# Two layers of attention and routed experts on one core: the sums between the layers move to GpSimd, and the gating work of layer 1 is spread over four units of its attention

## What is computed

```python
x = L0_attn_hidden_states                      # 4 x 512 x 256
xn = layernorm(x)
x = x + L0_attn(xn) + L0_ffn(xn)               # 16 experts, best 4 of each token, and a shared one
xn = layernorm(x)
x = x + L1_attn(xn) + L1_ffn(xn)               # 32 heads in 8 groups; 7 experts, best 3, and a shared one

# L1_attn, for each batch and each of 8 groups g with 4 heads of size 8
sim = q[g, r] @ k[g].T / sqrt(8)
out[g, r] = softmax(sim) @ v[g]
# L1_ffn: gating
probas = softmax(x @ gate_w + gate_b); take the best 3 of (probas + biases)
```

## Time and profile before

| | us |
|---|---|
| median of 3 runs | 1141.22 |
| the 3 runs | 1140.10, 1141.22, 1143.67 |
| span of the profiled execution, first to last instruction | 1136.1 |
| TensorE busy in it | 1018.1 (90%) |
| VectorE busy | 762.7 (67%) |
| ScalarE busy | 604.8 (53%) |
| GpSimd busy | 317.4 (28%) |

### The profile page before, as it was taken

One profiled execution on the slowest core, in us unless ns is written; L12 is line 12 of the kernel. 1 busy time (PEld: TensorE's weight loads), 2 busy tenths in 40 slices (PEclk: granted clock), 3 DMA queues, 4 the chain that ended last, 5 costly groups with the idle time before them and its releaser, 6 DMA issues.

```text
span 1136.1 us, 17535 instructions
## 1 busy us (share of the span) xinstructions
PE 1018.1 (90%) x5780; PEld 743.6 (65%) x5780; DVE 762.7 (67%) x1591; ACT 604.8 (53%) x911; POOL 317.4 (28%) x331
## 2 busy tenths in 40 slices
PE   4998898779999846799999999999999997999995
PEld 3877776669999724555555555555555565888884
DVE  6576454556655346798899888888888846444437
ACT  6325445355565543466665666666666665444431
POOL 2005777066655500000000122222221000455441
PEclk9999999989999967899999999999999998999999
DMA  6863333354444272011111222222222124333253
GB/s 231 315 263 126 124 110 120 113 195 150 136 124 135 89 305 35 14 28 29 29 29 29 43 55 57 56 56 57 56 56 43 63 73 155 108 108 101 92 196 137
DMA packets 49140, 120.49 MB, mean 106 GB/s; under 512 B 7752, under 2 KB 24904, under 8 KB 48520
## 3 DMA queue, kind: packets, MB, share of 16 engines
q1 hardware_dynamic: 36096, 82.80, 25.5%
q0 software_dynamic: 11808, 32.37, 7.5%
q10 hardware_dynamic: 1152, 4.19, 0.9%
HBM read 72.30 MB, written 52.42 MB: 110 GB/s over the span
## 4 chain that ended last, share of the span: by engine, by line
PE 65%; DVE 16%; POOL 7%; issue 4%; ACT 3%; DMA 3%; SPq 0%; ACTq 0%; DVEq 0%; POOLq 0%
PE psum L817 11%; PE psum L838 9%; PE psum L826 7%; DVE work_f L1699 6%; POOL xg L466 5%; PE psum L633 5%; PE psum L634 4%; PE psum L635 4%; PE psum L547 3%; PE psum L548 3%; PE psum L549 3%; PE psum L619 3%; PE psum L644 2%; DVE x L1310 1%; PE psum L665 1%
## 5 line engine op out<-in xcount | busy, mean ns | idle before, releaser
L1699 DVE TENSOR_REDUCE work_f<-psum 128x1 f32<-128x512 f32 x512 | 337.3, 685 | 49.1 <-PE psum L817 46.7
L1203 ACT ACTIVATE work_f<-psum 128x1024 f32<-128x1024 f32 x172 | 169.5, 1023 | 104.9 <-PE psum L826 100.5
L817 PE MATMUL psum<-work_r 128*128 128x512 f32 x512 | 207.8, 445 | 18.9 <-DVE work_f L1699 7.0
L473 POOL DMA_INDIRECT yk<-yb,dest x134 | 131.3, 980 | 240.1 <-ACT yb L1057 206.7
L817 PEld LDWEIGHTS psum<-work_r 128*128 128x128 f32 x512 | 93.4, 190 | 133.8 <-DVE work_f L1699 71.2
L826 PE MATMUL psum<-qm,work_r 128*128 128x512 f32 x512 | 160.8, 396 | 0.9 <-ACT work_f L1203 0.8
L466 POOL DMA_INDIRECT xg<-xn,slot x112 | 108.2, 966 | 180.9 <-PE psum L853 143.5
L826 PEld LDWEIGHTS psum<-qm,work_r 128*128 128x128 f32 x512 | 93.8, 188 | 24.1 <-ACT work_f L1203 6.2
L633 PE MATMUL psum<-wexp,xbh 128*128 x268 | 102.1, 381 | 7.4 <-issue 7.2
L1203 ACT ACTIVATE pt<-psum 128x1024 f32<-128x1024 f32 x84 | 82.8, 1022 | 45.9 <-PE psum L826 42.7
L634 PE MATMUL psum<-wexp,xbh 128*128 x268 | 96.4, 360 | 0.0
(11 more groups left out here) (218 smaller groups left out, 2065.2 us busy)
## 6 DMA issues: line engine op xcount, KB each, us to landing
xb<-xg SPq DMA_DIRECT2D x67, 258.0 KB
xg<-in_pad SPq DMA_DIRECT2D x1, 10320.0 KB
yg<-yk SPq DMA_DIRECT2D x20, 512.0 KB, 9.0
stage<-in_moe SPq DMA_DIRECT2D x16, 608.0 KB
xg<-in_pad SPq DMA_DIRECT2D x1, 7224.0 KB
work_r<-work_r SPq DMA_DIRECT2D x128, 48.0 KB
work_r<-work_r SPq DMA_DIRECT2D x32, 192.0 KB
stage<-in_moe SPq DMA_DIRECT2D x16, 384.0 KB, 3.7
```

The lines of the kernel that those rows point to most:

```text
L473: nc.gpsimd.indirect_dma_start(yk[l], bass.IndirectOffsetOnAxis(ap=dest[:, j % 8, i:i + 1], axis=0), yb[l][:, j % 2, i, :], None).then_inc ...
L817: nc.tensor.matmul(next_bank(pe, ("scores", n), b_mx, n + 1), qs[g % 2][:, t * P:(t + 1) * P], km[g % 4][:, r, :], start=True, stop=True). ...
L1203: nc.scalar.activation(pt[((b * NG + g) * QT + t) % 3][:, 2 * h:2 * h + 2, :], psum[:, 3 + 2 * h:5 + 2 * h, :], ACT.Exp, scale=float(HD) * ...
L1699: v.reduce_max(mx[:, s % 2, i:i + 1], ring["scores", n], AX.X).then_inc(b_mx, 1)
```

## The change

1. Batch 0: GpSimd adds choice 3 to choice 2; VectorE adds choices 0, 1 and then that sum to `x`.
2. Batch 1: as before, but TensorE's sum is made in two halves with `tokens_t(1, 0)` between them.
3. Batches 2 and 3: GpSimd makes four additions of 128 x 1024 each (`sum_choices`), the last onto `x`. TensorE's sums of these batches are gone.
4. All three projections of batch 0 stand one after the other ahead of stage (0, 0); ScalarE splits the first two before it normalises batch 1. VectorE's `root(1, 1)` stands behind its `clear()`.
5. The tokens' transposes of batches 2 and 3 are in the ring, one bank at a time, in stages (0, 1) and (0, 2); the logits of batches 0 to 3 and their transposes stand one batch at a time in stages (0, 0) to (0, 3). No stage waits for all of them. `lt[1]` holds two batches in place of four. The routing steps begin in stage (0, 4) and not in (0, 3).

```diff
+            def sum_choices(b):
+                y = yg[0][b]
+                pool.wait_ge(m_yg[b], 16 * TOP0)
+                nc.gpsimd.tensor_tensor(y[:, 1], y[:, 1], y[:, 2], ALU.add).then_inc(q_sum, 1)
+                nc.gpsimd.tensor_tensor(y[:, 3], y[:, 3], y[:, 0], ALU.add).then_inc(q_sum, 1)
+                pool.wait_ge(q_sum, choice_sums(b) - 1)
+                nc.gpsimd.tensor_tensor(y[:, 1], y[:, 1], y[:, 3], ALU.add).then_inc(q_sum, 1)
+                pool.wait_ge(q_sum, choice_sums(b))
+                tiles = slice(b * QT, (b + 1) * QT)
+                nc.gpsimd.tensor_tensor(x[:, tiles, :], x[:, tiles, :], y[:, 1], ALU.add).then_inc(q_x, 1)
-            for b in range(B):
-                root(1, b)
+            pool.wait_ge(m_yg[0], 16 * TOP0)
+            nc.gpsimd.tensor_tensor(yg[0][0][:, 2], yg[0][0][:, 2], yg[0][0][:, 3], ALU.add).then_inc(q_sum, 1)
+            root(1, 0)
+            pool.wait_ge(s_xb, TT)
+            pool.wait_ge(f_y, batches(0, B))
+            sum_choices(2)
+            root(1, 1)
+            sum_choices(3)
+            root(1, 2)
+            root(1, 3)
...
             # TensorE
-            sum_results(1, 4)
+            sum_results(0)
             tokens_t(1, 0)
-            sum_results(2, 6)
+            sum_results(1).then_inc(m_ps, 1)
             pe.wait_ge(s_split, SPLIT_A1)
             pe.wait_ge(s_xl, 2 * B + 2)
             project(2, 0, psum[:, 0, :])
             project(0, 0, psum[:, 2, :])
-            pe.wait_ge(s_ve, B + 2)
-            sum_results(3, 4)
-            pe.wait_ge(b_hi, 1)
-            tokens_t(1, 1)
+            project(1, 0, psum[:, 6, :])
+            pe.wait_ge(b_lo, 2)
...
-            stage(0, 0, False, {1: lambda: pe.wait_ge(s_xl, 2 * B + 4), 3: last_projection, 7: lambda: tokens_t(1, 2),
-                                11: lambda: tokens_t(1, 3), 12: first_values})
-            pe.wait_ge(s_xl, 2 * B + 8)
-            for b in range(B):
-                logits(1, b, psum[:, 4 + b, :])
-            logits_by_token(1)
-            pe.wait_ge(s_lc, 2)
-            stage(0, 1, False)
-            sequence(0, False)
+            stage(0, 0, False, {3: lambda: tokens_t(1, 1), 6: lambda: first_logits(0), 9: first_values,
+                                10: lambda: logits_by_token1(0), 13: lambda: first_logits(1)})
+            pe.wait_ge(s_xl, 2 * B + 4)
+            stage(0, 1, False, {1: lambda: logits_by_token1(1), 3: lambda: tokens_t1(2, 0), 6: lambda: tokens_t1(2, 1),
+                                14: lambda: first_logits(2)})
+            stage(0, 2, False, {3: lambda: tokens_t1(3, 0), 5: lambda: logits_by_token1(2), 6: lambda: tokens_t1(3, 1),
+                                14: lambda: first_logits(3)})
+            stage(0, 3, False, {5: lambda: logits_by_token1(3)})
...
             # ScalarE
             normalised(1, 0)
             high_parts(1, 0)
-            normalised(1, 1)
             compact(2, 0, psum[:, 0, :], 0)
             compact(0, 0, psum[:, 2, :], 1)
+            normalised(1, 1)
+            compact(1, 0, psum[:, 6, :], 2)
             high_parts(1, 1)
+            logits(1, 0, ring["logits", 0])
             normalised(1, 2)
+            logits(1, 1, ring["logits", 1])
+            act.wait_ge(q_sum, choice_sums(3))
+            stage(0, 1, False, {(0, 1): lambda: high_parts1(2, 0), (1, 0): lambda: high_parts1(2, 1),
+                                (3, 0): lambda: normalised(1, 3), (3, 1): lambda: logits(1, 2, ring["logits", 2])})
+            stage(0, 2, False, {(0, 1): lambda: high_parts1(3, 0), (1, 0): lambda: high_parts1(3, 1),
+                                (3, 1): lambda: logits(1, 3, ring["logits", 3])})
...
             # VectorE
-            combine0(0, 0)
+            dve.wait_ge(m_yg[0], 16 * TOP0)
+            add_choice(0, 0)
+            add_choice(0, 1)
+            dve.wait_ge(q_sum, 1)
+            add_choice(0, 2)
+            noted()
             moments(1, 0)
             root(1, 0)
-            combine0(1, 4)
+            dve.wait_ge(m_yg[1], 16 * TOP0)
+            add_choice(1, 0)
             low_parts(1, 0)
-            moments(1, 1)
-            root(1, 1)
+            dve.wait_ge(m_ps, sums(0, 1))
+            noted()
+            note(add_to_tokens(slice(QT, 2 * QT), 4))
...
             compact(2, 0, psum[:, 0, :], 0)
+            moments(1, 1)
             compact(0, 0, psum[:, 2, :], 1)
             clear()
             v.memset(rec[:], 0.0).then_inc(b_on, 1)
+            root(1, 1)
...
+            stage(0, 0, False, {4: lambda: compact(1, 0, psum[:, 6, :], 2), 6: lambda: low_parts(1, 1),
+                                8: lambda: moments_of(2), 11: lambda: root(1, 2),
+                                12: lambda: take_logits1(0), 14: lambda: values_by_key(0, psum[:, 7, :])})
+            stage(0, 1, False, {3: lambda: take_logits1(1), 5: lambda: low_parts1(2, 0), 8: lambda: low_parts1(2, 1),
+                                9: lambda: moments_of(3), 12: lambda: root(1, 3)})
+            stage(0, 2, False, {5: lambda: low_parts1(3, 0), 7: lambda: take_logits1(2), 8: lambda: low_parts1(3, 1)})
+            stage(0, 3, False, {7: gate})
```

More of the change, by code:

```diff
@@ L558, in tokens_t, with tokens_t1, logits_by_token1 @@
                     ins.then_inc(s_xnT, 1)
+            def tokens_t1(b, k):
+                pe.wait_ge(s_xn, TT + (b + 1) * QT)
+                o = next_bank(pe, ("tokens", b, k), s_xl, 2 * B + KH * b + k + 1)
+                for t in range(QT):
+                    ins = nc.tensor.transpose(o[:, t * P:(t + 1) * P], xn[1][:, b * QT + t, k * P:(k + 1) * P], ident)
+                ins.then_inc(s_xnT, 1)
+            def logits_by_token1(b):
+                pe.wait_ge(s_lt, B + b + 1)
+                o = next_bank(pe, ("logits by token", b), s_lc, 2 + b)
+                for t in range(QT):
+                    ins = nc.tensor.transpose(o[:, t * P:(t + 1) * P], lt[1][:, b % 2, t * P:(t + 1) * P], ident)
+                ins.then_inc(s_lx, 1)
             def logits(layer, b, o):
@@ L1008, in normalised, with high_parts1 @@
                                          bias=rs[:, 7, t:t + 1]).then_inc(s_xn, 1)
+            def high_parts1(b, k):
+                act.wait_ge(s_xnT, 2 * B + b * KH + k + 1)
+                copy(xt_hi[1][:, k, b * S:(b + 1) * S], ring["tokens", b, k]).then_inc(s_xh, 1)
             def logits(layer, b, o):
                 act.wait_ge(s_lg, layer * B + b + 1)
-                copy(lt[layer][:, b, :], o).then_inc(s_lt, 1)
+                if layer and b < 2:
+                    act.wait_ge(q_x, 1)
+                if layer and b >= 2:
+                    act.wait_ge(s_lx, b)
+                copy(lt[layer][:, b % 2 if layer else b, :], o).then_inc(s_lt, 1)
             def gating_exp(ne, count, n):
@@ L1188, in outputs, with stage @@
                 copy(ot[:], psum[:, 7, :]).then_inc(b_ot, 1)
-            def stage(b, s, last):
+            def stage(b, s, last, early={}):
                 back, following = s >= 1, not last and s >= 1
                 for t in range(QT):
-                    if isinstance(b, int) and (b, s, t) == (0, 2, 1):
-                        gating_exp(E1, 2, TT)
                     if back:
@@ L1208, in stage, with both @@
                     outputs(b, s - 1)
+            def both(*steps):
+                return lambda: [step() for step in steps]
             normalised(1, 0)
             high_parts(1, 0)
-            normalised(1, 1)
             compact(2, 0, psum[:, 0, :], 0)
             compact(0, 0, psum[:, 2, :], 1)
+            normalised(1, 1)
+            compact(1, 0, psum[:, 6, :], 2)
             high_parts(1, 1)
+            logits(1, 0, ring["logits", 0])
             normalised(1, 2)
-            compact(1, 0, psum[:, 3, :], 2)
-            high_parts(1, 2)
-            normalised(1, 3)
-            high_parts(1, 3)
-            for b in range(B):
-                logits(1, b, psum[:, 4 + b, :])
-            stage(0, 1, False)
-            for s in range(2, NG + 2):
+            logits(1, 1, ring["logits", 1])
[4 more added lines that the diff above has]
+                                (3, 1): lambda: logits(1, 3, ring["logits", 3])})
+            stage(0, 3, False, {(3, 0): lambda: gating_exp(E1, 2, TT)})
+            for s in range(4, NG + 2):
                 stage(0, s, False)
@@ L1507, in routed, with add_choice @@
                     weights(j)
-            def combine0(b, bank):
-                dve.wait_ge(f_y, batches(0, b + 1))
-                dve.wait_ge(s_xb, TT)
-                dve.wait_ge(m_yg[b], 16 * TOP0)
+            def add_choice(b, k):
                 tiles = slice(b * QT, (b + 1) * QT)
-                for k in range(1 if b else TOP0):
-                    noted()
-                    note(v.tensor_tensor(x[:, tiles, :], x[:, tiles, :], yg[0][b][:, k], ALU.add))
-                if b:
-                    dve.wait_ge(m_ps, sums(0, b))
-                    noted()
```

(15 more changed lines are left out.)

80 lines of the change are left out of this document (44 added, 36 removed).

## The result

The changed kernel takes 1146.6 us in the median of 5 runs (1145.55 to 1148.22) against 1140.1 of the kernel before (5 runs, 1138.75 to 1143.67). The ratio is 1.0057, with a 95% interval of 1.0043 to 1.007: slower, and above the range of 1131 to 1145. The span of the profiled execution went from 1136.1 to 1143.7 us. What lies around the instructions is 1.8 us (1145.55 for the execution with the span of 1143.7), not the 5.1 given ahead of the prediction, so the profiled execution of before took an estimated 1137.9 and was a quick one: the 7.6 us between the spans are more than the 6.5 between the medians.

What follows compares the result with a forecast made beforehand. VectorE's sums, statistics and low parts were taken to set the first stage, then a wait for TensorE's gating block. Head +1.6, stage (0, 0) -7.7, block and later stages summed to -3.3 us: 1137.9 from 1141.2, range 1131 to 1145.

Steps and rivals of the forecast that it cites:

- Step 1: Batch 0's additions: three on VectorE and one on GpSimd, one after the other, take 6.1 us; costs 1.1.
- Step 2: Batch 0's statistics and roots up to the projections: TensorE projects at 425.7, before 426.1.
- the toss: Whether batch 0's last root instruction, due at 418.4, passes GpSimd's additions from 418.3; if caught, 2.2 to 4.5 us later.
- Step 3: Head, projections: the key split no longer stands behind 2.08 us of ScalarE; first score at 437.0, before 438.6.
- Step 4: End of head: VectorE's root of batch 1 waits on GpSimd's additions, 6.5 us; first maximum at 441, before 439.4.
- Step 5: Stage (0, 0): takes 19 us, its last maximum at 460, before 466.1.
- case D: Rival: nine places in the three-bank ring cost 2.0 us each; stages (0, 1) to (0, 3) over 52, total 1146; chance 0.15.
- Step 7: Stage (0, 2): added tokens and logits cost 3.0 us, bounds 1.4 and 5.4; ends at 493.3, before 497.7.
- step 8: Stage (0, 3): 14.4 us, ending at 507.6, before 511.4; routing steps paid one stage later, 0.5.
- Step 6: Stage (0, 1): 17.0 us, 1.0 of it waiting for ScalarE's copy; ends at 477.0, before 484.4.
- B: Rival: VectorE is let in beside GpSimd's additions, so the first maximum comes 4.5 us sooner; 1133.5; chance 0.23.
- C: Rival: batch 0's root is caught at 418.4 and held to 423.2, +3.5 us; 1141.5, no change seen; chance 0.18.

Runs made afterwards that it cites:

- e1_hold: The changed kernel, but GpSimd waits for VectorE's roots of batches 0 and 1 before its next sums; 1.0013 of the kernel before.
- e7_logits: The changed kernel with only the logits' copies of batches 2 and 3 moved ahead of ScalarE's exponential (3, 0); 1.0032 of the kernel before.
- e6_tokens: The changed kernel with only the first token copy of batches 2 and 3 moved ahead of ScalarE's exponential (0, 0); 1.003 of the kernel before.
- e5_three: The changed kernel with GpSimd waiting for VectorE's roots, the exponential table loaded early, and token and logits copies ahead of the exponentials; 0.9933 of the kernel before.
- e11_no_logits: e5_three without the logits of batches 2 and 3, their turned form, copies and additions; 0.9911 of the kernel before.

## Why the prediction was wrong, step by step

**Step 1, right.** Batch 0's additions ended 5.87 us after the landing (6.1 predicted). The timeline of after, head:

```profile
408.08 2.34 POOL L542 TENSOR_TENSOR yg<-yg 128x1024 f32<-128x1024 f32 x1 [9.63 <-DMA yg<-yk]
408.22 5.87 DVE L1572 TENSOR_TENSOR x<-x,yg 128x1024 f32<-128x1024 f32 x3 [16.61 <-DMA yg<-yk]
...
418.25 3.36 POOL L533 TENSOR_TENSOR yg<-yg 128x1024 f32<-128x1024 f32 x1 [0.98 <-DMA yg<-yk]
...
432.43 2.34 POOL L533 TENSOR_TENSOR yg<-yg 128x1024 f32<-128x1024 f32 x1
433.84 0.95 DVE L1337 TENSOR_TENSOR rs<-rs 128x4 f32<-128x4 f32 x1
434.73 2.35 POOL L534 TENSOR_TENSOR yg<-yg 128x1024 f32<-128x1024 f32 x1
434.83 2.27 DVE L1338 TENSOR_TENSOR rs<-rs 128x4 f32<-128x4 f32 x1
...
437.13 0.17 DVE L1339 TENSOR_SCALAR rs<-rs 128x4 f32<-128x4 f32 x1
437.16 2.35 POOL L536 TENSOR_TENSOR yg<-yg 128x1024 f32<-128x1024 f32 x1
437.34 2.19 DVE L1340 TENSOR_TENSOR rs<-rs 128x4 f32<-128x4 f32 x1
439.56 0.16 DVE L1341 SCALAR_TENSOR_TENSOR rs<-mv,rs 128x4 f32<-128x4 f32 x1
439.64 2.48 DVE L1760 TENSOR_REDUCE work_f<-psum 128x1 f32<-128x512 f32 x4
```

**Step 2, right in the toss, 2.2 us off in the size.** The root was through before GpSimd's addition, and `add_choice` started 0.08 us ahead of it, at 418.17; here it was GpSimd that stood (3.36 us in place of 2.35). So TensorE projected at 423.5 and not at 425.7. That is 0.7 us beyond the text's case "1.5 earlier", in which `add_choice` gets in between two additions; that it could start ahead of both was not considered.

**Step 3, right but for a wait not named.** The key's low part, at 427.47, was itself held by GpSimd (1.95 us for 0.7). The first score came at 436.19 (437.0).

**Step 4, right in kind.** The root of batch 1 took 433.84 to 439.72, 5.9 us where I put 6.5. Three of its instructions of 128 x 4 elements ended with a GpSimd addition each: 0.95, 2.27 and 2.19 us. The `SCALAR_TENSOR_TENSOR` behind the last of them took 0.16. The Trainium skill has the rule behind it (SBUF — State Buffer, section "Who interferes with whom": the port pair is an exclusive lock), and this trace agrees, with 2.27 and 2.19 us for instructions that take 0.16 in e1_hold. That the first maximum came at 439.64 and not at 441 has two halves: the root began 0.6 us earlier than forecast (433.84, not 434.4), and took 0.6 us less. e1_hold shows what the step's wait costs at the end of the head: 2.6 us.

**Step 5, right.** 18.9 us against 19, at a granted clock of 0.68.

**Steps 6 to 8 failed.** I had 17.0 + 16.3 + 14.4 = 47.7; the stages took 20.2 + 23.4 + 16.7 = 60.3, 12.6 more, past the mark of 52 that the text set for case D, the ring. The runs split the 12.6 as follows:

- 3.8 for the logits' copies behind the exponential (e7_logits). Step 7 named this very wait at 1.1 us for batch 2, from the exponential's length; undoing it was worth 1.9, and step 8's for batch 3, "half taken in by the slack", another 1.9.
- 2.7 for the tokens' copies (e6_tokens). Step 6 had 1.0 for one of them, step 7 nothing.
- 3.6 for TensorE's clock (e1_hold). For these stages the text named it only in (0, 1), and only as what would make the forecast fail, "at 18 or more"; that stage took 20.2 at 0.81. It priced no fall in (0, 2).
- 0.9 for the table load (e5_three). "The exponential table is loaded once as before" is true of the count, but in the kernel before it was loaded at 470.95, while ScalarE had nothing else to do in the block, and here a copy that frees a bank stood behind it. The timeline of before:

```profile
470.95 1.28 ACT L1203 ACT_TABLE_LOAD   x1
477.17 3.04 ACT L1203 ACTIVATE work_f<-psum 128x1024 f32<-128x1024 f32 x3 [4.93 <-PE psum L826]
```

- 1.6 in (0, 2) beyond the 3.0 by the projections' rows: 17.9 against 16.3 with everything in order, which no run splits further. In (0, 1) and (0, 3) the order and the early table make my numbers about true (16.6 for 17.0, 14.8 for 14.4).

So the step that failed is the sizing of the waits in the ring, in steps 6 to 8: the forecast put them at 1.0 us in step 6, 1.1 in step 7 and half of one in step 8, where they cost 6.5, and put nothing for the table load and the clock, which cost 4.5 more. The places themselves were put too low as well: in good order the three stages took 49.3 us, 1.6 more than my 47.7, which already had those 2.6 us of waits in it. Even my upper bounds, 17.0 - 1.0 + 2.5 = 18.5 for (0, 1) and 13.25 + 5.4 = 18.7 for (0, 2), were passed, and at the clock of e1_hold too (18.8 and 21.2). I priced each place by itself, while one cause, ScalarE's order, pushed all of them to the same end. Case D had 0.15, took 2.0 for each of nine places and gave 1146: its size was right, partly by luck, since its reason holds only in part. The four places of the logits of batches 2 and 3 cost 1.3 to 1.4 each in good order (e11_no_logits), the low end of the price taken; half of the 12.6 (3.8 + 2.7) came not from the places but from who frees them.

**Step 8's routing** (0.5) is right: stages (0, 4) to (0, 6) together took 45.3 us against 44.6 before. What lies behind (0, 6) took 579.6 us against 580.1, so the carrying over one for one was right too.

The rivals: B is out (the stand-off is there at 2.27 and 2.19 us), C is out (the toss passed), D happened, with the reason only in part its own.

## What to carry to other kernels

When work is moved into a ring of few banks, follow the engine that frees each bank and not only the one that fills it: what stands ahead of the copy in its fixed order, an exponential that waits for the bank's own producer above all, is paid by everyone. Several waits that hang on one engine's order are one uncertainty and go to the same end together, so a range made of their separate middles is too narrow. TensorE's clock is a risk beside them that these waits alone don't decide: with the same waits in stage (0, 2) it was 0.85 in one kernel and 1.00 in another, for 2.2 us. Spreading a block to fill slack paid here only when the order was then set anew: one wait, one early table load and four copies moved, with no work removed, turned 1.0057 into 0.9933. With the sums left to TensorE and VectorE the good order gave 0.9987, no difference to before that can be told, and with GpSimd's sums but the old block 1.002: it took both.
